# Layer 1's scores for three quarters of the rows: dots on VectorE in place of turns and a four-column product on TensorE

## The chip, the cores and the metric

The kernel runs on one core of a Trainium2 chip. The metric is the device time of one execution in microseconds (us). The core has four compute engines that work side by side, each with its own in-order program: TensorE (PE, products and turns), VectorE (DVE), ScalarE (ACT) and GpSimd (POOL). SyncE (SP) issues DMAs. The engines wait for one another through semaphores.

## The reference, cut to what matters

Four graph layers run one after the other over the same adjacency matrix `adj` (4096 x 4096, f32) and node features `x` (4096 x 128). Each layer normalises the rows of `x`, applies its own operation, and adds the result to `x`.

```python
h = relu(layernorm(x)); x = x + L0(h, adj)       # (inv_deg * A') @ h, a linear map, relu
h = relu(layernorm(x)); x = x + L1(h, adj)       # graph attention, 2 heads
...
# L1, head i; x here is h above
x_norm = ln(x, g1, b1)
h = x_norm @ ff0_w[i].T
s_src = h @ attn_w[i, :c];  s_dst = h @ attn_w[i, c:]
e = leaky_relu(s_src[:, None] + s_dst[None, :])
att = softmax(where(mask, e, NEG), axis=1) @ h + x
```

So every row of layer 1 needs four scores: s_src and s_dst for two heads. Each is linear in the normalised row, so the kernel folds ff0_w, attn_w, g1 and b1 into one 128 x 4 matrix and multiplies each normalised row of 128 values by its four columns. The last of the 128 places carries the constant that b1 needs.

## The kernel before, in words

The 4096 rows are T = 32 blocks of 128, in Q = 4 quarters of S = 8 blocks. A layer works through the quarters. For a quarter `q`, TensorE does 32 steps `k` (function `run`, line 466). In layer 0 a step is 8 products of a 128 x 128 piece of `adj_t` with the 129 columns of block `k` (line 366). Each step's 512 KB of `adj_t` are loaded by SP (line 287) into a ring: 8 places in the first three quarters (`FIRST`), 4 places in the last quarter (`STREAM`), which lie in `ring` and share their space with what layer 1 uses (R in place 0, the tiles E in places 1 to 3).

The load of step k waits until TensorE has used step k-8 (k-4 in the last quarter) and until VectorE has made the mask of that step. VectorE's `masks` (lines 1152 to 1160) writes for each step a uint8 tile that says where `adj_t` is above 0.

All that is not a product or a mask is a hook: a small piece of work that an engine does behind the products or the mask of a given step `k`, in an order written out by hand. In layer 0's quarter q, VectorE's hooks are the rest of quarter q-1's layer 0 (`post0`: divisors, own part, bias, add, self-loops) and its preparation for layer 1 (`feed(1, ...)`: statistics and scales of two normalisations). `stage0` at line 1217 gives their places.

ScalarE writes the normalised rows of quarter q-1 into G[:, 1] (signal `f_norm`). Then, in the kernel before, TensorE turns the 8 blocks (hook 19, line 409), ScalarE copies them from PSUM to U (line 647), TensorE multiplies each by the four columns `qcol` (hook 22, line 420), and ScalarE copies the result into `score1` (line 703, signal `f_placed`).

The last quarter of layer 0 has three things more. VectorE takes the largest score of the first three quarters at step 26 (`early_of`, line 1018). TensorE spreads it over the partitions at hook 25, after a wait for it (`spread_top`, line 453). From it come biases, exponentials on ScalarE, and a spread of rows at TensorE's hook 28 (`spread_rows`). VectorE scales two quarters of G behind the masks 30 and 31 (line 1094). Then layer 1 begins: VectorE makes a tile E for each step (line 1124) and TensorE multiplies it with G (line 382). The scores of the fourth quarter are made in layer 1's first quarter, in the same manner, at TensorE's hooks 17 and 18 of that quarter.

`spare` is the fifth place of `ring`, and holds small weights. `w0T` (layer 0's weights) is its first 128 columns and is not needed after the first quarter; `ff0raw` and `w2raw` lie in the 384 columns behind the other weights, and `affine` and `proj2` lie over parts of them. V is a work tile of 8 x 128 that ScalarE and VectorE share.

Of the kernel before, what the change touches and what calls it, by code (L numbers as in the profile page):

```python
# [64 lines left out]
def graph_layers(nc, x, adj, adj_t, diag, alpha, w0_t, bias0, ff0, ff0_t, ff1_t, attn, g1, b1, g2, b2,  # L65
# [20 lines left out]
    with ExitStack() as ctx:  # L86
# [40 lines left out]
        ff0raw = [spare[:, o + h * D:o + (1 + h) * D] for h in range(HEADS)]  # L127
        affine = ff0raw[1]
        w2raw = spare[:, o + 2 * D:o + 3 * D]
        proj2 = spare[:, o:o + D + 2]  # L130
        mean2 = spare[:, o + D + 2:o + 2 * D + 2]
        fold, later = [spare[:, o + 3 * D + i * S:o + 3 * D + (i + 1) * S] for i in range(2)]
# [52 lines left out]
        f_var, f_dev, f_scale, f_norm = sem("f_var"), sem("f_dev"), sem("f_scale"), sem("f_norm")  # L185
        f2_var, f2_dev, f2_scale, f2_in = sem("f2_var"), sem("f2_dev"), sem("f2_scale"), sem("f2_in")
        h_turned, h_wide, h_projected, h_placed = sem("h_turned"), sem("h_wide"), sem("h_projected"), sem("h_placed")
        f_turned, f_wide, f_projected, f_placed = sem("f_turned"), sem("f_wide"), sem("f_projected"), sem("f_placed")

        top_placed, top_spread, bias_made, row_shifted = sem("top_placed"), sem("top_spread"), sem("bias_made"), sem("row_shifted")  # L190
# [78 lines left out]
        @block.sync  # L269
        def _(sp):  # L270
            def load_x(t, n, loaded):
                sp.dma_start(X[:, t:t + n, :], x[t * P:(t + n) * P, :].rearrange("(s p) d -> p s d", p=P)).then_inc(loaded, 16)  # L272

            def layer0(q, some=range(T)):

                L = STREAM if last_of(q) else FIRST
                for k in some:
                    if k >= L:
                        sp.wait_ge(slot_used, q * (T - 1) + k - L + 1)
                        sp.wait_ge(mask_made, q * T + k - L + 1)  # L280
                    elif 0 < q < Q - 1:
                        if k == L - 1:
                            sp.wait_ge(acc_summed[NB - 1], q)
                        else:
                            sp.wait_ge(slot_used, q * (T - 1) + k - L + 2)
                        sp.wait_ge(mask_made, q * T + k - L + 1)
                    sp.dma_start(tile0(q, k), span(adj_t[k * P:(k + 1) * P, :], q * QC, QC)).then_inc(loaded0(q, k)[0], 16)

            def layer3(q):

                for k in range(T):
                    if not fixed(q):
                        if k == T - 1:
                            sp.wait_ge(acc_summed[NB - 1], q + 2 * Q)
                        else:
                            sp.wait_ge(deep_used, (q - 1) * (T - 1) + k + 1)
                    sp.dma_start(stream3[:, k, :], span(adj[k * P:(k + 1) * P, :], q * QC, QC)).then_inc(deep_loaded[k], 16)

            load_x(0, S // 2, x_first)
            load_x(S // 2, S // 2, x_loaded[0])  # L300
            sp.dma_start(w0T, w0_t).then_inc(w0_loaded, 16)
            layer0(0, range(2))
            load_x(S, S, x_loaded[1])
            layer0(0, range(2, STREAM))
            load_x(2 * S, S, x_loaded[2])
            load_x(3 * S, S, x_loaded[3])
            layer0(0, range(STREAM, T))
            for q in range(1, Q):
                layer0(q)


            sp.wait_ge(back_summed, 1)
            sp.dma_start(proj2[:, 0:D], w2).then_inc(w2_loaded, 16)


            sp.wait_ge(saved, 16 * Q)

            def bring_back(q):
                if fixed(q):
                    sp.wait_ge(post_done, 2 * Q)  # L320
                else:
                    sp.wait_ge(f_turned, q + 2 * Q)
                sp.dma_start(V[:, :, :].rearrange("p s d -> p (s d)"), span(inputs1, q * QC, QC)).then_inc(back, 16)
            bring_back(0)
            quarters(sp, 1, Q - 1, bring_back)

            sp.wait_ge(e_made, 3 * Q * T)
            layer3(0)
            quarters(sp, 1, Q - 1, layer3)
            for b in range(NB):  # L330
                sp.wait_ge(last_made, b + 1)
                some = slice(3 * b, 3 * b + width(b))
                sp.dma_start(out.rearrange("(t p) d -> p t d", p=P)[:, (Q - 1) * S:, :][:, some, :], V[:, some, :])\
                    .then_inc(stored, 16)
            sp.wait_ge(stored, 16 * (Q - 1 + NB))
# [21 lines left out]
        def _(pe):  # L357
# [41 lines left out]

            def feed(h, p, weights, wide, spreads, posts):  # L400

                at = p if h < 3 else p - Q

                def turned():
                    pe.wait_ge(f_norm, p + 1)
                    wait(pe, rows_kept, spreads)
                    if h == 1:
                        for s in range(S):
                            mm = pe.transpose(turn[:, s * P:(s + 1) * P], G[:, 1, (p - Q) * S + s, 0:P], ident[:, :])
                    else:  # L410
                        mm = turn_v()
                    mm.then_inc(f_turned, 1)

                def project():
                    pe.wait_ge(f_wide, at + 1)
                    wait(pe, f_placed, at)
                    wait(pe, post_done, posts)
                    for s in range(S):
                        dst = mix[:, 0, s * 4:s * 4 + 4] if h == 1 else mix[:, s // 3, (s % 3) * PW:(s % 3) * PW + wide]
                        mm = pe.matmul(dst, U[:, s * P:(s + 1) * P], weights, start=True, stop=True, skip_group_check=True)  # L420
                    mm.then_inc(f_projected, 1)
                return turned, project
# [111 lines left out]
                pe.matmul(mix[:, 2, 0:4], affine, qv[:, 0:4], start=True, stop=True, skip_group_check=True)\  # L534
                    .then_inc(back_summed, 1)

            def stage0(q, more={}):
                turned, project = feed(1, Q + q - 1, qcol, 4, 0, q)
                run(0, q, {19: turned, 22: project} | more)
            stage0(1, {3: turn_weights_back, 21: lambda: pe.wait_ge(back_placed, 1)})  # L540
            for q in range(2, Q - 1):
                stage0(q)
            stage0(Q - 1, {25: lambda: spread_top(early_top[1]), 28: lambda: spread_rows(0)})


            def spread_fold():
# [21 lines left out]
            def stage2(q):  # L568
# [6 lines left out]
                if last_of(q):  # L575
                    ks = [1, 11, 12, 25, 26, 27, 29]  
                    run(2, q, at(ks, steps + (lambda: spread_top(early_top[3]), lambda: spread_rows(m))))
                else:
                    ks = [1, 13, 15, 26, 29, 27]  
                    run(2, q, at(ks, steps + (lambda: spread_rows(m, q + 2 * Q),)))  # L580
            stage2(0)
            pe.wait_ge(qv2_placed, 1)
            quarters(pe, 1, Q - 2, stage2)
# [28 lines left out]
        def _(act):  # L612
# [47 lines left out]
            def feed(h, p, q, between=()):  # L660
# [14 lines left out]
                else:  # L675
# [9 lines left out]
                    if h == 1:  # L685
# [1 line left out]
                        act.wait_ge(f2_scale, q + 1)  # L687
                        normalise(lambda s: blocks(G[:, 1, :, :], q, 1, s)[:, 0, 0:D - 1], lambda s: V[:, s, 0:D - 1],
                                  local(scale), local(shift), ACT.Identity, f_norm)
                at = p if h < 3 else p - Q  # L690
                if fixed(p) and p == 0:
                    first_halves()
                    return
                if h == 3:
                    wait(act, half_summed, 0 if fixed(q) and q == 0 else q * 1)
                    widen(f_turned, at + 1, f_wide, halves=True)
                else:
                    widen(f_turned, at + 1, f_wide)
# [153 lines left out]
                feed(0, q, q)  # L852

            def post0(q):
                act.wait_ge(f_turned, q + Q)
                settle()
                act.activation(V[:, :, :], blocks(G[:, 0, :, :], q)[:, :, 0:D], ACT.Copy, scale=restc).then_inc(own_made, 1)
                take(q, later=False)
# [82 lines left out]
        @block.vector  # L941
        def _(dve):
            st = Steps(dve, dve_step)
            STAGE0, STAGE1, STAGE2, STAGE3 = 20, 6, 12, 7
            V3 = V[:, :, :]
            Uf = U3[:, :, 0:D]
            Ud = U3[:, :, D]
# [37 lines left out]
            def feed(h, p, q):  # L985
# [7 lines left out]
                def input_ready():  # L993
                    dve.wait_ge(f2_in, q + 1)

                def second_scales():
                    scales(f2_dev, q + 1, f2_scale, keep=(2, q))

                def halves():
                    dve.wait_ge(f_wide, p - Q + 1)  # L1000
                    wait(dve, half_summed, 0 if fixed(q) and q == 0 else q * 1)
                    dve.scalar_tensor_tensor(hmean, hpart[0], hpart[1], hmean, ALU.add, ALU.add).then_inc(half_summed, 1)
                steps = statistics(lambda s: blocks(X, q, 1, s)[:, 0, :], f_var) + [first_scales]
                if h == 1:
                    half, rest = statistics(of_v, f2_var)
                    steps += [lambda: (input_ready(), half()), rest, second_scales]
                if h == 3:
                    steps += [halves]
                return steps
# [163 lines left out]
            def place_back():  # L1173
# [4 lines left out]
                for c, i in enumerate((1, 3, 0, 2)):  # L1178
                    ins = dve.tensor_copy(qcol[:, c:c + 1], mix[:, 2, i:i + 1])
                ins.then_inc(back_placed, 1)  # L1180
            masks(0, at([0, 1, 2, 6, 7, 9, 14, 15, 17], own_feed(1) + own_feed(2) + own_feed(3)))
            prepare()
            dve.wait_ge(consts_made, 1)
# [32 lines left out]

            def stage0(q, more={}):
                post, fed = post0(q - 1), feed(1, q - 1 + Q, q - 1)
                masks(q, at([2, 3, 5, 6, 18, 7, 8, 10, 12, 13, 15], post + fed) | more)
            stage0(1, {4: place_back})  # L1220
            quarters(dve, 2, Q - 2, stage0, st, STAGE0)
            early = early_of(1)
            stage0(Q - 1, {26: early[0], 28: early[1], 30: lambda: scale_g(1, 0), 31: lambda: scale_g(1, 1)})
# [206 lines left out]
```

## Time and profile before

| | us |
|---|---|
| median of 3 runs | 1242.03 |
| lowest and highest run | 1241.24 and 1245.62 |
| the profiled execution | 1240.94 |
| its span in the trace | 1239.1 |
| PE busy in the span | 1223.0 (99%) |
| DVE busy | 752.7 (61%) |
| ACT busy | 317.8 (26%) |
| layer 0's last three quarters, in the trace | about 79 to 260 |

The profile page is one profiled execution. It gives the busy time of each engine, the chain of work that ended last, the costliest groups of instructions by line, and the DMA issues. A product of f32 shows as two PE instructions. The trace behind it gives each instruction with its start and duration; consecutive instructions of an engine overlap by part of their durations, so the mean duration of one and the distance from one start to the next are two numbers.

### The profile page before, as it was taken

What the parts mean: (1) busy time and instruction counts of PE and PEld (TensorE: products, weight loads), DVE (VectorE), ACT (ScalarE), POOL (GpSimd) and SP (SyncE); (2) the same over time, 40 slices, a digit from 0 to 9 for tenths busy, and PEclk for the clock granted to TensorE, in tenths of its full rate; (3) what the DMA queues carried; (4) which work ended last, traced back from release to release, by engine and by line L of the source; (5) the groups of instructions that cost most, each with busy time, mean ns of one, the idle gap of its engine ahead of it and who ended that gap; (6) DMA issues with size and microseconds to landing.
All of it is one profiled execution on the core that took longest, in us unless ns stands there. A gap on an engine that the chain in (4) does not pass through costs nothing.

```text
span 1239.1 us, 20060 instructions
## 1 busy us (share of the span) xinstructions
PE 1223.0 (99%) x7953; PEld 967.4 (78%) x7953; DVE 752.7 (61%) x1359; ACT 317.8 (26%) x769; POOL 9.6 (1%) x21
## 2 busy tenths in 40 slices
PE   8999999999999999999999999899999999999998
PEld 8999999964444444444454547899999999999998
DVE  5446554588877777778878787778787840000001
ACT  3312121234433324231424144442312130000000
POOL 3000000000000000000000000000000000000000
PEclk9999999999999999999999999999999999999999
DMA  9888886820000000000000000000000069999810
GB/s 315 275 268 285 281 278 215 275 73 1 17 1 17 0 18 0 17 17 1 1 17 0 17 0 18 1 1 1 1 0 1 1 242 409 410 410 398 294 62 18
DMA packets 47241, 144.33 MB, mean 116 GB/s; under 512 B 4784, under 2 KB 13248, under 8 KB 47168
## 3 DMA queue, kind: packets, MB, share of 16 engines
q1 hardware_dynamic: 42976, 139.08, 31.3%
q10 hardware_dynamic: 3696, 3.67, 0.8%
q8 instruction: 52, 0.85, 0.3%
q0 software_dynamic: 496, 0.55, 0.2%
q14 instruction: 21, 0.17, 0.0%
HBM read 139.09 MB, written 4.19 MB: 116 GB/s over the span
## 4 chain that ended last, share of the span: by engine, by line
PE 87%; DVE 7%; DMA 2%; issue 1%; ACT 1%; SPq 1%; DVEq 0%; ACTq 0%
PE acc L366 51%; PE acc L382 30%; DVE ring L1124 4%; PE mix L420 2%; PE mix L448 1%; PE mix L435 1%; PE turn L397 1%; PE turn L393 1%; ACT V L623 1%; DMA mask<-in_adj_t 1%; SPq L272 1%; DMA mask<-in_adj 1%; DVE stats L960 1%; DVE stats L956 0%; DVE X L1273 0%
## 5 line engine op out<-in xcount | busy, mean ns | idle before, releaser
L1124 DVE SCALAR_TENSOR_TENSOR ring<-ring,score,mask 128x1024 f32<-128x1024 f32 x384 | 482.9, 1281 | 113.1 <-PE acc L382 69.5
L382 PE MATMUL acc<-ring,G 128*128 128x512 f32 x1024 | 450.5, 594 | 3.2 <-DVE ring L1124 2.7
L366 PE MATMUL acc<-G,mask 128*128 128x129 f32 x3584 | 403.5, 275 | 1.6 <-DMA mask<-in_adj 1.1
L366 PEld LDWEIGHTS acc<-G,mask 128*128 128x128 f32 x3584 | 401.5, 192 | 2.1 <-DMA mask<-in_adj 1.5
L382 PEld LDWEIGHTS acc<-ring,G 128*128 128x128 f32 x1024 | 189.3, 190 | 234.0 <-issue 201.5
L366 PE MATMUL acc<-G,ring 128*128 128x129 f32 x2560 | 289.8, 275 | 0.3 <-DVE ring L1124 0.3
L366 PEld LDWEIGHTS acc<-G,ring 128*128 128x128 f32 x2560 | 287.8, 192 | 1.5 <-DVE ring L1124 1.2
L1158 DVE TENSOR_SCALAR mask<-mask 128x1024 uint8<-128x1024 f32 x96 | 64.5, 689 | 53.7 <-DMA mask<-in_adj_t 53.5
L1375 DVE TENSOR_SCALAR zero<-U 128x8 f32<-128x8 f32 x3 | 0.5, 171 | 155.0 <-ACT U L816 155.0
L816 ACT COPY U<-acc 128x387 f32<-128x387 f32 (+1 forms) x36 | 15.6, 446 | 270.9 <-PE acc L366 269.9
L635 ACT ACTIVATE dev<-var 128x8 f32<-128x8 f32 x28 | 5.9, 210 | 266.6 <-DVE var L969 266.6
L1158 DVE TENSOR_SCALAR mask<-ring 128x1024 uint8<-128x1024 f32 x32 | 22.0, 692 | 32.1 <-DMA ring<-in_adj_t 22.2
L623 ACT ACTIVATE V<-X,shift,scale 128x128 f32<-128x128 f32 (+1 forms) x92 | 36.7, 481 | 0.0
L775 ACT COPY ring<-turn 128x512 f32<-128x512 f32 x14 | 8.2, 585 | 109.2 <-DVE ring L1124 64.3
L619 ACT ACT_TABLE_LOAD x26 | 33.4, 1283 | 1.2 <-PEq L1409 0.8
L615 ACT COPY cols<-ident 128x1 f32<-128x1 f32 x40 | 7.6, 190 | 95.8 <-DVE shift L979 35.6
L1394 DVE SCALAR_TENSOR_TENSOR zero<-U 128x3 f32<-128x3 f32 (+1 forms) x3 | 0.5, 161 | 50.8 <-ACT U L816 50.8
L623 ACT ACTIVATE V<-U,shift,scale 128x128 f32<-128x128 f32 x64 | 25.5, 481 | 10.3 <-DVE shift L979 10.3
L420 PEld LDWEIGHTS mix<-ring,U 128*128 128x128 f32 x176 | 20.8, 192 | 2.0 <-issue 1.2
L397 PEld LDWEIGHTS turn<-ident,V 128*128 128x128 f32 x120 | 13.7, 141 | 10.0 <-ACT V L623 5.8
L420 PE MATMUL mix<-ring,U 128*128 128x4 f32 (+2 forms) x176 | 21.0, 265 | 0.0
L397 PE MATMUL turn<-ident,V 128*128 128x128 f32 x120 | 15.7, 274 | 4.1 <-ACT V L623 4.1
(168 smaller groups left out, 548.2 us busy)
## 6 DMA issues: line engine op xcount, KB each, us to landing
mask<-in_adj SPq DMA_DIRECT2D x128, 512.0 KB, 14.9
mask<-in_adj_t SPq DMA_DIRECT2D x96, 512.0 KB, 4.7
ring<-in_adj_t SPq DMA_DIRECT2D x32, 512.0 KB, 4.7
inputs<-V ACTq DMA_DIRECT2D x4, 512.0 KB, 2.7
V<-inputs SPq DMA_DIRECT2D x4, 512.0 KB, 3.9
X<-in_x SPq DMA_DIRECT2D x3, 512.0 KB, 10.6
out_x<-V ACTq DMA_DIRECT2D x3, 512.0 KB, 15.1
X<-in_x SPq DMA_DIRECT2D x2, 256.0 KB, 3.2
```

Source lines behind the costliest of these rows:

```text
L272: sp.dma_start(X[:, t:t + n, :], x[t * P:(t + n) * P, :].rearrange("(s p) d -> p s d", p=P)).then_inc(loaded, 16)
L366: mm = pe.matmul(acc[:, b, (s % 3) * DW:(s % 3) * DW + DW], lhs[:, s * P:(s + 1) * P], g, start=(k == 0 and s % 3 == 0), stop=(k == T - 1) ...
L382: mm = pe.matmul(acc[:, c, :], g, moving[:, c * BANK:(c + 1) * BANK], start=(k == 0), stop=(k == T - 1), skip_group_check=True)
L393: return pe.transpose(dst, col.broadcast_to([P, P]), ident[:, :])
L397: mm = pe.transpose(turn[:, s * P:(s + 1) * P], V[:, s, :], ident[:, :])
L420: mm = pe.matmul(dst, U[:, s * P:(s + 1) * P], weights, start=True, stop=True, skip_group_check=True)
L435: mm = pe.matmul(mix[:, s // 3, (s % 3) * DW:(s % 3) * DW + DW], U[:, s * P:(s + 1) * P], back_w[h], start=True, stop=True, skip_group_che ...
L619: act.activation(warm[func], ident[:, 0:1], func)
L623: ins = act.activation(dst(s), src(s), func, bias=add(s), scale=mul(s))
L816: act.copy(U[:, b * 3 * DW:b * 3 * DW + w], acc[:, b, 0:w]).then_inc(acc_taken, 1)
L1124: dve.scalar_tensor_tensor(E[k % EB], R, rank[h][:, k:k + 1], span(mask, (q * T + k) * QC, QC), ALU.max, ALU.mult).then_inc(e_made, 1)
L1158: dve.tensor_scalar(span(mask, (q * T + k) * QC, QC), tile0(q, k), 0.0, None, ALU.is_gt).then_inc(mask_made, 1)
```

## The change

For the quarters 0, 1 and 2 the scores are no longer made by TensorE. VectorE makes them from the rows in G[:, 1] with `scalar_tensor_tensor`: it multiplies the 128 values of a row with the 128 values of one score's column, and sums along the row with `accum_out` into `score1`. That is one instruction for each block and score, 4 x 8 = 32 for a quarter, in four hooks of eight at the steps 18, 20, 21 and 23. The elementwise product goes to V and is not read. The fourth quarter's scores are made as before.

The four columns have to lie along the free axis on all partitions. In layer 0's quarter 1, TensorE spreads them (four transposes of a broadcast column, hook 6), and VectorE copies them into `w0T` and the 384 columns of `spare` (hook 9). The self-loops move from hook 18 to hook 22. The waits that counted `f_turned`, `f_wide` and `f_placed` of layer 1's feeds are renumbered, and the load of `w2` waits for the last dots rather than for `back_summed`.

```diff
+        dot_w = [w0T] + [spare[:, o + i * D:o + (i + 1) * D] for i in range(3)]
...
-            sp.wait_ge(back_summed, 1)
+            sp.wait_ge(f_placed, 2 * Q - 1)
             sp.dma_start(proj2[:, 0:D], w2).then_inc(w2_loaded, 16)
...
-            def stage0(q, more={}):
-                turned, project = feed(1, Q + q - 1, qcol, 4, 0, q)
-                run(0, q, {19: turned, 22: project} | more)
-            stage0(1, {3: turn_weights_back, 21: lambda: pe.wait_ge(back_placed, 1)})
+            def spread_dots():
+                pe.wait_ge(back_placed, 1)
+                for c in range(4):
+                    mm = spread(qcol[:, c:c + 1], mix[:, 0, c * P:(c + 1) * P])
+                mm.then_inc(dots_spread, 1)
+            run(0, 1, {3: turn_weights_back, 6: spread_dots})
             for q in range(2, Q - 1):
-                stage0(q)
-            stage0(Q - 1, {25: lambda: spread_top(early_top[1]), 28: lambda: spread_rows(0)})
+                run(0, q, {})
+            run(0, Q - 1, {25: lambda: spread_top(early_top[1]), 28: lambda: spread_rows(0)})
...
             def post0(q):
-                act.wait_ge(f_turned, q + Q)
+                act.wait_ge(f_placed, q + Q)
...
+                def dots(c):
+                    if c == 0:
+                        dve.wait_ge(f_norm, p + 1)
+                    else:
+                        st.wait()
+                    for s in range(S):
+                        ins = dve.scalar_tensor_tensor(V[:, s, :], blocks(G[:, 1, :, :], q, 1, s)[:, 0, 0:D], 1.0, dot_w[c],
+                                                       ALU.mult, ALU.mult, accum_out=blocks(score1, q, 1, s)[:, 0, c:c + 1])
+                    if c == 3:
+                        ins.then_inc(f_placed, 1)
+                    else:
+                        st.mark(ins)
...
+            def keep_dots():
+                dve.wait_ge(dots_spread, 1)
+                dve.tensor_copy(w0T, mix[:, 0, 0:P])
+                dve.tensor_copy(spare[:, o:o + 3 * D], mix[:, 0, P:4 * P]).then_inc(dots_kept, 1)
+                dve.wait_ge(dots_kept, 1)
...
-                masks(q, at([2, 3, 5, 6, 18, 7, 8, 10, 12, 13, 15], post + fed) | more)
-            stage0(1, {4: place_back})
+                masks(q, at([2, 3, 5, 6, 22, 7, 8, 10, 12, 13, 15, 18, 20, 21, 23], post + fed) | more)
+            stage0(1, {4: place_back, 9: keep_dots})
```

## Rows read from the trace of the kernel before

**Rows 1.** The page: engines' busy time, TensorE's granted clock by slice.
```profile
PE 1223.0 (99%) x7953; PEld 967.4 (78%) x7953; DVE 752.7 (61%) x1359; ACT 317.8 (26%) x769; POOL 9.6 (1%) x21
...
PEclk9999999999999999999999999999999999999999
```

**Rows 2.** Windows, layer 0's last three quarters: PE, PEld, DVE, ACT, POOL busy; clock, DMA share, GB/s.
```profile
80.00:139.00 59.00, 59.00 (x531) 59.00 (x530) 33.04 (x94) 12.51 (x35) 0.00 (x0) 1.00 0.83 277
139.00:199.20 60.20, 60.20 (x542) 60.20 (x541) 30.90 (x84) 13.60 (x39) 0.00 (x0) 1.00 0.78 267
199.20:260.40 61.20, 61.20 (x547) 60.98 (x546) 37.74 (x96) 16.39 (x44) 0.00 (x0) 1.00 0.73 242
```

**Rows 3.** The chain in order of time, last quarter of layer 0: start, length, what.
```profile
235.38 0.87 PE turn L409 x8
...
241.62 1.68 PE mix L420 x16
243.30 5.46 PE acc L366 x48
248.76 0.11 PE mix L393
...
252.48 4.83 DMA ring<-in_adj_t
```

**Rows 4.** Timeline of VectorE in the last quarter: start, length, instruction, idle before.
```profile
199.44 1.90 DVE L1158 TENSOR_SCALAR mask<-ring 128x1024 uint8<-128x1024 f32 x3 [9.78 <-PE acc L366]
...
230.94 0.69 DVE L1158 TENSOR_SCALAR mask<-ring 128x1024 uint8<-128x1024 f32 x1 [0.93 <-DMA ring<-in_adj_t]
231.55 1.70 DVE L1213 TENSOR_TENSOR mask<-mask,ident 128x128 uint8<-128x128 uint8 x8
...
246.70 0.19 DVE L1018 TENSOR_REDUCE cols<-score 128x1 f32<-128x24 f32 x1
...
257.94 1.22 DVE L1094 TENSOR_TENSOR G<-G 128x1024 f32<-128x1024 f32 x1
259.07 2.47 DVE L1124 SCALAR_TENSOR_TENSOR ring<-ring,score,mask 128x1024 f32<-128x1024 f32 x2
```

**Rows 5.** Timeline of ScalarE in the last quarter.
```profile
227.18 3.18 ACT L623 ACTIVATE G<-V,shift,scale 128x127 f32 x8 [2.46 <-DVE norms L982]
```

**Rows 6.** Groups by line: count, busy us, mean ns of one, idle before.
```profile
L1202 DVE TENSOR_TENSOR U<-U,ring 128x1024 f32<-128x1024 f32 x4 | 4.9, 1220 | 1.6 <-ACT U L623 1.6
L1198 DVE SCALAR_TENSOR_TENSOR U<-U,cols,V 128x1024 f32<-128x1024 f32 x4 | 5.1, 1277 | 0.0
L1205 DVE SCALAR_TENSOR_TENSOR X<-U,X 128x1024 f32<-128x1024 f32 x4 | 4.9, 1218 | 0.0
```

**Rows 7.** Timeline of VectorE: eight 128 x 128 operations with two f32 sources.
```profile
1065.22 2.19 DVE L1383 SCALAR_TENSOR_TENSOR V<-U,inv,X 128x128 f32<-128x128 f32 x8
```

**Rows 8.** Timeline of ScalarE: activations that sum along the row, with the sum's read.
```profile
619.03 0.60 ACT L643 ACTIVATE U<-turn 128x512 f32<-128x512 f32 x1 [1.59 <-PE turn L397]
619.52 0.19 ACT L643 ACTIVATION_READ_ACCUMULATOR U<-turn 128x1 f32 x1
619.61 0.59 ACT L643 ACTIVATE U<-turn 128x512 f32<-128x512 f32 x1
```

**Rows 9.** Timeline of VectorE in the quarters 1 and 2.
```profile
87.35 0.34 DVE L1179 COPY ring<-mix 128x1 f32<-128x1 f32 x4
...
162.52 2.07 DVE L1158 TENSOR_SCALAR mask<-mask 128x1024 uint8<-128x1024 f32 x3
```

**Rows 10.** Timeline of ScalarE in quarter 2.
```profile
162.74 3.18 ACT L623 ACTIVATE G<-V,shift,scale 128x127 f32 x8 [1.68 <-DVE norms L982]
```

**Rows 11.** Timeline of TensorE in quarters 1 and 2, and its longest wait later.
```profile
86.64 28.83 PE L366 MATMUL acc<-G,mask 128*128 128x129 f32 x256
...
175.14 1.04 PE L409 MATMUL turn<-ident,G 128*128 128x128 f32 x8
...
802.36 1.09 PE L397 MATMUL turn<-ident,V 128*128 128x128 f32 x8 [2.75 <-ACT V L623]
```

More of the change, by code:

```diff
@@ L187, in graph_layers @@
         h_turned, h_wide, h_projected, h_placed = sem("h_turned"), sem("h_wide"), sem("h_projected"), sem("h_placed")
+        dots_spread, dots_kept = sem("dots_spread"), sem("dots_kept")
         f_turned, f_wide, f_projected, f_placed = sem("f_turned"), sem("f_wide"), sem("f_projected"), sem("f_placed")
@@ L321, in bring_back @@
                 else:
-                    sp.wait_ge(f_turned, q + 2 * Q)
+                    sp.wait_ge(f_turned, q + Q + 1)
                 sp.dma_start(V[:, :, :].rearrange("p s d -> p (s d)"), span(inputs1, q * QC, QC)).then_inc(back, 16)
@@ L400, in feed @@
             def feed(h, p, weights, wide, spreads, posts):
-                at = p if h < 3 else p - Q
+                at = p if h == 0 else Q if h == 1 else p - 2 * Q + 1
                 def turned():
@@ L415, in project @@
                     pe.wait_ge(f_wide, at + 1)
-                    wait(pe, f_placed, at)
+                    wait(pe, f_placed, p if h < 3 else p - Q)
                     wait(pe, post_done, posts)
@@ L579, in stage2 @@
                     ks = [1, 13, 15, 26, 29, 27]
-                    run(2, q, at(ks, steps + (lambda: spread_rows(m, q + 2 * Q),)))
+                    run(2, q, at(ks, steps + (lambda: spread_rows(m, q + Q + 1),)))
             stage2(0)
@@ L689, in feed @@
                                   local(scale), local(shift), ACT.Identity, f_norm)
-                at = p if h < 3 else p - Q
                 if fixed(p) and p == 0:
@@ L693, in feed @@
                     return
+                if h == 1 and not (fixed(p) and p == 2 * Q - 1):
+                    return
+                at = p if h == 0 else Q if h == 1 else p - 2 * Q + 1
                 if h == 3:
@@ L943, in _ @@
             st = Steps(dve, dve_step)
-            STAGE0, STAGE1, STAGE2, STAGE3 = 20, 6, 12, 7
+            STAGE0, STAGE1, STAGE2, STAGE3 = 23, 6, 12, 7
             V3 = V[:, :, :]
@@ L999, in halves @@
                 def halves():
-                    dve.wait_ge(f_wide, p - Q + 1)
+                    dve.wait_ge(f_wide, p - 2 * Q + 2)
                     wait(dve, half_summed, 0 if fixed(q) and q == 0 else q * 1)
@@ L1006, in feed @@
                     steps += [lambda: (input_ready(), half()), rest, second_scales]
+                if h == 1 and not (fixed(p) and p == 2 * Q - 1):
+                    steps += [lambda c=c: dots(c) for c in range(4)]
                 if h == 3:
```

## The prediction

> **What bounds the kernel now.** I read the page first. TensorE is busy for 1223.0 us of the 1239.1 us span, and its granted clock is full in all forty slices [rows 1]. The windows of layer 0's last three quarters say the same of the place of the change: PE fills them, while VectorE has 33.04, 30.90 and 37.74 us in 59.00, 60.20 and 61.20 [rows 2]. So what leaves TensorE's stream there shortens the kernel, as long as nothing makes TensorE wait in its place. The chain in order of time shows what leaves: in each quarter one piece of 0.87 us (eight turns) and one of 1.68 us (eight products, two instructions each), both on the chain [rows 3]. The chain also shows where layer 0 ends: at 252.48 it goes from TensorE to the load of step 31 (4.83 us), then by its mask and the scaling of G to VectorE's first tile E at 259.07 [rows 3, 4]. From there VectorE holds the chain for a while. A shift of TensorE's step 27, which frees that load, is therefore a shift of all that follows. Last I read VectorE's timeline in the last quarter, because it has the most to do there and the ring has only four places.
>
> **TensorE's part.** Removed: three times 0.87 + 1.68 = 2.55 us, together 7.65 us. Added: four transposes of a broadcast column, each as long as the one at 248.76, 0.11 us [rows 3]: 0.44 us. Net 7.21 us less. The four wait for `back_placed` at hook 6 of quarter 1. VectorE places the last column at 87.35 + 0.34 = 87.69; TensorE starts step 4 at 86.64 and has 256 instructions in 28.83 us, 1.80 a step of sixteen, so it comes to the hook at 92.0 [rows 9, 11]. The wait is hidden with 4.3 us to spare. `keep_dots` needs the result only behind mask 9, and its two copies go into VectorE's slack of this quarter.
>
> ScalarE loses two copies and one small copy a quarter; it is idle for three quarters of the time there, so this is worth nothing. SP's `w2` load now waits for the last dots, but SP is still issuing layer 0's last loads then (the one at 252.48 is later [rows 3]), and nothing asks for `w2` before layer 2.
>
> **What one dot costs.** The trace has no sum along the row on VectorE. Its nearest rows: eight `scalar_tensor_tensor` of 128 x 128 with two f32 sources take 2.19 us at 346 ns each, so one starts (2.19 - 0.346) / 7 = 0.263 us behind the other [rows 7]. Those take a scalar from memory; at 1024 columns such an operation takes 1277 ns and one with an immediate 1218 [rows 6], and the dots have an immediate: 0.263 - 0.059 = 0.204. The sum has to be written out. On ScalarE that is an instruction of its own: it starts at 619.52 and the next activation at 619.61, 0.09 us [rows 8]. A dot is then 0.204 + 0.09 = 0.29 us, my value, and eight are 2.32. The low end is 0.204, if the sum is free. The high end is a dot with no overlap at all: 0.346 + 0.19 (the full length of ScalarE's read) = 0.54. I take the low side, since every pipelined row of VectorE has the overlap.
>
> The Trainium skill ("VectorE: DVE Perf Modes", The DRAIN you can't avoid) says that a next operation doesn't start until the pipe is empty. Rows 7 contradict this for plain operations (2.19 us, not 8 x 0.346 = 2.77); for a pair of dot and read no row speaks, and by that rule the kernel would end near the slower rival below.
>
> **Quarters 1 and 2: hidden.** VectorE gets 32 dots, 9.3 us, and has 26 to 29 us idle [rows 2]. It waits for `f_norm` at step 18: in quarter 2 its mask 18 ends at about 163.9 (the second of the three at 162.52), and ScalarE ends the rows at 162.74 + 3.18 = 165.92 [rows 9, 10], so it stands for 2 us, with the masks from 19 on queued behind it. From 165.92, three hooks (6.96), five masks (3.0) and the self-loops (1.6) put mask 23 at 177.5. TensorE, which began the turns behind step 19 at 175.14 [rows 11], would end step 23 without them at about 182.3. The load of step 31 asks for both; TensorE is the later. Even a dot of 0.49 us would only make them equal, and eight places leave seven more steps. So both quarters give their full 2.55 us. The loads then have to come at 512 KB in 1.8 us, 291 GB/s, where the windows have 277 and 267 [rows 2] because the 2.55 us are in them.
>
> **The last quarter: not hidden.** All times here in the clock of the kernel before. VectorE's mask 18 starts when its load has landed, 230.94; `f_norm` is there already (227.18 + 3.18 = 230.36 [rows 5]). From here to the largest score VectorE must do, in order: nine masks (18 to 26) at (1.90 - 0.69) / 2 = 0.605, 5.45 us; four hooks of dots, 32 d for a dot of d us; the self-loops, 1.61 (1.70 less the overlap of 0.09 with the next start); and the reduction with its handover, 0.19 + 0.05 [rows 4]. It is done at 238.24 + 32 d, with d = 0.29 at 247.52. The loads do not hold it: that of step 26 asks for mask 22 (240.93) and lands 4.83 us later at 245.8, and VectorE gets to it at 246.7.
>
> TensorE ended step 25 at 243.30 + 5.46 = 248.76. Less 2.55 this is 246.21, and here it waits for the largest score [rows 3]. The stall is 238.24 + 32 d - 246.21 = 32 d - 7.97, which is 1.31 us. Before, this wait was covered: the reduction started at 246.70, 2.1 us early. Behind it nothing new is late: the load of step 28 asks for mask 24 (246.07), lands at 250.9, and TensorE gets there at 251.2. The end of layer 0 and the first tile E move with TensorE's steps 26 and 27. The last quarter gives 2.55 - 1.31 = 1.24 us.
>
> **Sum.** -7.65 + 0.44 + 1.31 = -5.9 us. In the profiled execution's own time, 1240.94 - 5.9 = 1235.0. The median of the three runs is 1.1 us above that execution, so the forecast of a median is 1236.1. In general the change is 32 d - 15.2 us while the stall is positive, that is from d = 0.25 on: -7.2 (the floor) up to there, -4.6 for d = 0.33, -3.7 for 0.36, +2.1 for the high end 0.54.
>
> **Rivals.**
> 1. *No stall.* If a dot takes 0.25 us or less, VectorE has the score in time and all 7.2 us are gained: 1234.8. For it: the low end 0.204 and the ScalarE read's 0.09 being perhaps less here (four 128 x 1 copies take 0.34 us, of which one is 0.146: 0.065 apart [rows 9]; that gives 0.27). Against: even that leaves 0.6 us of stall. Chance 12%.
> 2. *The sum takes an own pass or a second cycle for each element.* From 128 to 1024 columns the start distance grows by about 1.03 ns a column (1.19 us at 1024, from 2.47 - 1.28 in rows 4, and 0.263 at 128), so 128 columns are 0.13 us; doubled, d = 0.42 and the change is -1.7 us: 1240.3. Against it: at 1024 columns the two-source operation that multiplies and adds takes no longer (1218 ns) than the plain one (1220) [rows 6], but neither sums. Chance 15%.
> 3. *Slower: the dots do not overlap.* Each dot waits for the whole one before it and its read: 0.346 + 0.146 (a single 128 x 1 copy [rows 9]) = 0.49 us, and the stall at step 25's hook is 7.7 us, more than all three quarters give back. The change is +0.5: 1242.5; the point from which it decides is d = 0.475. With rival 2 on top, d = 0.62 and +4.6: 1246.6. For it: the read needs the end of the sum before it. Against: ScalarE's read needs the same and costs 0.09 us. Chance 10%.
> 4. *TensorE's clock falls in the new stall.* The longest wait of TensorE, 2.75 us at 799.6, left the clock full [rows 1, 11], and the stall that I expect is half of that. If it falls for two steps, these cost double, +3.6: 1239.7. Chance 3%.
>
> On rival 2 the Trainium skill ("Vector Engine (DVE) Microarchitecture Reference", Points that are easy to get wrong) says that this form with two non-bf16 SBUF sources runs at half rate, as no port is left to read back the accumulator. The 1218 ns show that it doesn't for operations without a sum; for one with a sum no row here tells. By it the sum would be rival 2's.
>
> **How the numbers follow.** The forecast has the other 60%, with d from 0.26 to 0.36 and a change of -6.9 to -3.7. A measurement can tell about 0.5%, 6.2 us. That is beyond d = 0.28: rival 1 whole, and a good third of the forecast's cases, make 35% for faster. Rivals 2 and 4, most of 3 and the rest make 60% for the same. Slower by 6.2 us needs a dot near 0.67 us or something unforeseen: 5%. The range goes from the floor with a little for the spread of the medians, 1233.8, up to 1241.0, which takes in rival 2 and leaves rival 3 out.
>
> **What would show it.** Right: no L409 and 16 fewer L420 instructions in each of the three quarters; windows of PE 2.5 us shorter in quarter 2; dots of about 0.29 us each, eight in 2.3; one wait of TensorE of 1 to 2 us before the spread at step 25 of the last quarter, put down to VectorE's reduction. Wrong: waits of TensorE for loads in quarters 1 and 2 (then masks are late there), a wait at hook 6, the first tile E later against the last product than now, or dots of over 0.4 us.

## The result, and the profile after

| | before | changed |
|---|---|---|
| median of 8 runs, us | 1242.38 | 1235.58 |
| lowest and highest | 1240.58 to 1245.62 | 1231.05 to 1238.30 |
| profiled execution, us | 1240.94 | 1234.05 |
| its span, us | 1239.1 | 1232.3 |
| ratio to before, with its 95% interval | | 0.9941 [0.9926, 0.9957] |

The changed kernel is faster: by 0.59% (7.3 us) by the ratio of the runs, by 6.8 us by the medians. The forecast was 1236.1 us, a change of -5.9.

The page of the changed kernel, engines' busy time:

```profile
PE 1217.1 (99%) x7885; PEld 961.8 (78%) x7885; DVE 772.2 (63%) x1553; ACT 314.0 (25%) x760; POOL 9.6 (1%) x21
```

TensorE has 5.9 us less and VectorE 19.5 us more [rows 1]. Windows over layer 0's last three quarters (columns as in rows 2). The edge at 139.00 is where quarter 1 ends in the kernel before; here it ends about 2 us earlier, so the second window holds that quarter's gain too:

```profile
80.00:139.00 59.00, 59.00 (x531) 59.00 (x530) 41.13 (x167) 12.10 (x34) 0.00 (x0) 1.00 0.85 289
139.00:194.50 55.50, 55.50 (x499) 55.50 (x498) 36.25 (x143) 11.63 (x33) 0.00 (x0) 1.00 0.79 276
194.50:253.20 58.70, 58.44 (x522) 58.06 (x520) 43.86 (x160) 15.05 (x41) 0.00 (x0) 1.00 0.74 253
```

TensorE still fills the windows. Its timeline at the start of the last quarter, at its new wait and at the start of layer 1:

```profile
194.41 46.62 PE L368 MATMUL acc<-G,ring 128*128 128x129 f32 x416
241.28 0.32 PE L395 MATMUL mix<-ident,cols 128*128 128x128 f32 x1 [0.26 <-DVE cols L1040]
...
253.22 5.46 PE L384 MATMUL acc<-ring,G 128*128 128x512 f32 x12
```

In the kernel before, the last quarter starts at 199.24 and layer 1 at 260.40. So 4.83 us are gained up to the last quarter, which took 61.2 us and takes 58.8. The chain in order of time (start, length, what):

```profile
92.30 0.44 PE mix L395 x4
92.73 142.95 PE acc L368 x1280
...
235.69 4.71 DMA ring<-in_adj_t
...
240.43 0.69 DVE mask L1180
241.12 0.11 DVE cols L1040
...
241.28 0.32 PE mix L395
...
243.42 4.96 DMA ring<-in_adj_t
...
251.89 2.48 DVE ring L1146 x2
```

Three things can be read here. The four spreads cost 0.44 us. From 92.73 TensorE does 80 steps in one piece of 142.95 us, where pieces of 0.87 and 1.68 us stood in between [rows 3]. And in the last quarter the chain leaves TensorE for the load of step 26 (235.69), its mask and the reduction, before the spread of the largest score. Of TensorE's waits in the whole kernel one is new (us in total, times, longest), and one is gone, 1.15 us for a load of layer 3:

```profile
PE mix L395 <- DVE cols L1040: 0.3, 1, 0.3
```

VectorE's timeline in the last quarter, at the first hook of dots and at the largest score (start, length, and in brackets the idle time before):

```profile
226.03 0.70 DVE L1180 TENSOR_SCALAR mask<-ring 128x1024 uint8<-128x1024 f32 x1 [0.73 <-DMA ring<-in_adj_t]
226.64 0.29 DVE L1009 SCALAR_TENSOR_TENSOR V<-G,ring 128x128 f32<-128x128 f32 x1
226.85 0.08 DVE L1009 DVE_READ_ACCUMULATOR V<-G,ring 128x1 f32 x1
226.85 0.29 DVE L1009 SCALAR_TENSOR_TENSOR V<-G,ring 128x128 f32<-128x128 f32 x1
...
228.34 0.69 DVE L1180 TENSOR_SCALAR mask<-ring 128x1024 uint8<-128x1024 f32 x1
...
240.43 0.69 DVE L1180 TENSOR_SCALAR mask<-ring 128x1024 uint8<-128x1024 f32 x1 [0.45 <-DMA ring<-in_adj_t]
241.04 0.19 DVE L1040 TENSOR_REDUCE cols<-score 128x1 f32<-128x24 f32 x1
```

Eight dots take 228.34 - 226.64 = 1.70 us, 0.213 us each. Each dot is two instructions, and the read of the sum starts at the same time as the next dot: it hides beneath it. Before the mask of step 26 VectorE is idle for 0.45 us, until the load has landed: it is not VectorE's work that makes the score late.

### The profile page after: what moved, and what is told of

It reads as the page before. It is cut to its first block, busy times and chain, and to the rows that moved or that the text cites. A ratio compares the mean times of both kernels' runs of the same rounds, so it can differ in the third digit from the quotient of the medians.

```text
span 1232.3 us, 20107 instructions
## 1 busy us (share of the span) xinstructions
PE 1217.1 (99%) x7885; PEld 961.8 (78%) x7885; DVE 772.2 (63%) x1553; ACT 314.0 (25%) x760; POOL 9.6 (1%) x21
## 4 chain that ended last, share of the span: by engine, by line
PE 87%; DVE 7%; DMA 2%; issue 1%; ACT 1%; SPq 1%; DVEq 0%; ACTq 0%
PE acc L368 52%; PE acc L384 30%; DVE ring L1146 4%; PE mix L450 1%; PE turn L399 1%; PE mix L437 1%; PE mix L422 1%; PE turn L395 1%; DMA mask<-in_adj_t 1%; DMA ring<-in_adj_t 1%; ACT V L627 1%; DVE stats L966 1%; SPq L274 1%; DVE stats L962 0%; DVE X L1300 0%
## 5 line engine op out<-in xcount | busy, mean ns | idle before, releaser
L1009 DVE SCALAR_TENSOR_TENSOR V<-G,ring 128x128 f32<-128x128 f32 x96 | 21.3, 287 | 2.7 <-ACT G L627 2.7
L627 ACT ACTIVATE U<-U,inv 128x128 f32<-128x128 f32 x64 | 19.5, 388 | 0.0
```

The source lines that it names most:

```text
L627: ins = act.activation(dst(s), src(s), func, bias=add(s), scale=mul(s))
L1009: ins = dve.scalar_tensor_tensor(V[:, s, :], blocks(G[:, 1, :, :], q, 1, s)[:, 0, 0:D], 1.0, dot_w[c], ALU.mult, ALU.mult, accum_out=block ...
```

## The experiments

Each was timed beside the kernel before on one chip, so the ratios are what is compared. One thousandth is 1.24 us. Each ratio has an interval of 1.4 to 2 us to either side, so the last column, a difference of two ratios, is uncertain by about 2 us.

| kernel | median, us | ratio to before [95%] | against the changed kernel, by ratio |
|---|---|---|---|
| changed | 1235.58 | 0.9941 [0.9926, 0.9957] | |
| e1, TensorE's work put back | 1243.92 | 1.0020 [1.0008, 1.0032] | +9.8 us |
| e2, no dots | 1234.75 | 0.9944 [0.9931, 0.9958] | +0.4 |
| e3, dots twice in the last quarter | 1242.14 | 0.9999 [0.9986, 1.0011] | +7.2 |
| e4, dots twice in quarters 1, 2 | 1234.78 | 0.9947 [0.9932, 0.9961] | +0.7 |
| e5, all four quarters as dots | 1239.81 | 0.9981 [0.9970, 0.9992] | +5.0 |
| e6, hooks moved in the last quarter | 1233.83 | 0.9936 [0.9923, 0.9948] | -0.6 |
| e7, e6 and the turn one step later | 1231.91 | 0.9921 [0.9905, 0.9936] | -2.5 |
| e8, no sum | 1233.15 (one run) | | |

**e1: TensorE's removed work put back.**

```diff
+            def turns_again(q):
+                pe.wait_ge(f_norm, Q + q)
+                ...  # eight transposes of G[:, 1] into turn
+            def products_again(q):
+                pe.wait_ge(dots_kept, 1)
+                ...  # eight products of G[:, 1] with qcol into mix
+            def again(q):
+                return {19: lambda: turns_again(q), 22: lambda: products_again(q)}
-            run(0, 1, {3: turn_weights_back, 6: spread_dots})
+            run(0, 1, {3: turn_weights_back, 6: spread_dots} | again(1))
...          # and the same for the quarters 2 and 3
```

> The changed kernel with TensorE's removed work put back as idle work: at steps 19 and 22 of layer 0's quarters 1 to 3 it turns eight blocks of G[:, 1] and does the eight four-column products again (from G in place of U), and nobody reads them. The dots stay and give the scores. My theory (the gain is the 2.55 us a quarter that left TensorE's stream): time comes back by 7.65 us less the 0.26 us stall that the products then cover, so 7.4 us above the changed kernel and 0.4 above the kernel before (the four spreads). Rival (the gain comes from ScalarE's freed copies or from the moved self-loops and waits): it stays near the changed kernel, within 2 us.

Measured: 9.8 us above the changed kernel and 0.2% above the one before. Its chain in the last quarter, and VectorE's first tile E:

```profile
235.65 0.87 PE turn L547 x8
...
241.89 1.68 PE mix L552 x16
...
252.75 5.06 DMA ring<-in_adj_t
```

```profile
259.57 2.47 DVE L1159 SCALAR_TENSOR_TENSOR ring<-ring,score,mask 128x1024 f32<-128x1024 f32 x2
```

The first tile E comes at 259.57: 7.68 us later than in the changed kernel (251.89) and 0.50 later than before [rows 4]. This is close to the theory's 7.4 and 0.4. So what layer 0 gains is the 2.55 us a quarter; ScalarE's relief and the moved self-loops, which e1 keeps, give nothing that shows there. The time lost 2 us more than that. In this profiled execution they lie near 1007, where TensorE waits for an early load of layer 3, and the granted clock is 0.70 in the window from 1008 to 1012:

```profile
1009.61 10.59 PE L368 MATMUL acc<-G,mask 128*128 128x129 f32 x78 [2.08 <-DMA mask<-in_adj]
```

The kernel before has this wait too (1.15 us). None of the eight profiled executions without TensorE's turns and products in layer 0 has it, neither the changed kernel nor e2 to e8. So 1 to 2 us of the gain may lie there, outside the prediction's sum. One execution of each kernel can't settle it, and why the load is later was not tried.

**e2: no dots.**

```diff
-                    for s in range(S):
-                        ins = dve.scalar_tensor_tensor(V[:, s, :], ..., accum_out=...)
+                    ins = dve.memset(blocks(score1, q)[:, :, c], 0.0)
```

> The changed kernel with each hook of eight dots replaced by one memset of eight zeros into the score column, so the scores of three quarters are left out and VectorE has 20 us less. As the prediction put it, the dots cost a stall of 1.3 us in the last quarter: this kernel would be 1.3 us faster. My present theory (trace of the changed kernel: a dot starts 0.213 us behind the other, the wait at step 25 is 0.26 us and ends with the load of step 26): it is the same as the changed kernel, within 0.3 us, and the wait of 0.26 us at the spread of the largest score is still there, since the ring of four places sets it.

Measured: the same time as with the dots. The wait at the spread is still there; in this execution it is 0.45 us, and TensorE had waited 0.62 us for a load five steps before:

```profile
241.88 0.32 PE L395 MATMUL mix<-ident,cols 128*128 128x128 f32 x1 [0.45 <-DVE cols L1038]
```

The times alone, uncertain by 2 us, could not tell 1.3 us from nothing; the traces can. With the dots VectorE is idle before the mask of step 26, and without them the wait is no shorter: the prediction's 1.3 us for the dots are refuted, and what is left of the stall belongs to the loads of the ring of four places. How much is left differs from execution to execution, though the ring, its loads and the hook are the same: 0.26 us in the changed kernel, 0.45 here, 0.17 in e5, none in e4 and e8.

**e3 and e4: the dots twice, in the last quarter or in the two before it.**

```diff
-                    for s in range(S):
+                    for again in range(2 if fixed(q) and q == Q - 2 else 1):     # e4: if not (...)
+                        if again:
+                            st.then(ins)
+                        for s in range(S):
```

> The changed kernel with each dot of the last quarter of layer 0 done twice (64 in place of 32), so that a dot costs 0.43 us there. Theory (VectorE's stretch from mask 18 to the largest score decides, by 32 d): the stretch takes 5.45 + 1.61 + 0.24 + 64 x 0.213 = 20.9 us from 226.03, the score comes at 247.0, TensorE waits 5.9 us at step 25 and the loads of steps 25 and 26 in front of it take part of that; time 5.0 to 6.0 us above the changed kernel. Rival (VectorE is idle enough, and the work is hidden): 0 to 1 us.

> The changed kernel with each dot of layer 0's quarters 1 and 2 done twice, the last quarter as it is. Theory (eight places in the ring, VectorE ahead of TensorE by 5 us and more): 0, within 0.5 us. Rival (VectorE's masks become late and the loads with them): 2 to 6 us slower, with waits of TensorE for loads in both quarters.

Measured: +7.2 us and +0.7 us. In e4 VectorE is busy 43.27 of the 55.6 us in the window of quarter 2, up from 36.25 of 55.5, and TensorE has no wait in either quarter:

```profile
92.83 102.00 PE L368 MATMUL acc<-G,mask 128*128 128x129 f32 x912
```

```profile
139.00:194.60 55.60, 55.60 (x501) 55.60 (x500) 43.27 (x209) 11.46 (x33) 0.00 (x0) 1.00 0.83 294
```

The extra dots are hidden. In e3 the stall is there as worked out; TensorE's timeline and three windows from the end of the stall on (columns as in rows 2):

```profile
247.45 0.47 PE L395 MATMUL mix<-ident,cols 128*128 128x128 f32 x1 [5.51 <-DVE cols L1043]
247.72 7.17 PE L368 MATMUL acc<-G,ring 128*128 128x129 f32 x48
```

```profile
247.50:249.50 2.00, 2.00 (x10) 2.00 (x11) 0.49 (x1) 0.00 (x0) 0.00 (x0) 0.50 0.90 313
249.50:251.50 2.00, 2.00 (x13) 2.00 (x13) 1.22 (x5) 0.08 (x1) 0.00 (x0) 0.59 0.49 193
251.50:253.50 2.00, 2.00 (x21) 2.00 (x20) 0.72 (x2) 0.58 (x3) 0.00 (x0) 1.00 0.46 119
```

The wait is 5.51 us against 5.9 less a part. Behind it the granted clock is 0.50, TensorE's lower level, and three steps take 7.17 us where they take 5.52 at full clock: 1.65 us that the expectation did not have. This is the prediction's fourth rival, at a stall four times as long as the one it was put for. With it the expected 5 to 6 us become the measured 7. So 32 more dots in the last quarter cost 7 us, and 64 more in the two quarters before it cost nothing that can be measured: it is the place that decides.

**e5: the fourth quarter as dots too.**

```diff
-                if h == 1 and not (fixed(p) and p == 2 * Q - 1):
+                if h == 1:
                     steps += [lambda c=c: dots(c) for c in range(4)]
...
-                    ks = [17, 18, 19, 21, 22, 25, 26]
-                    run(1, q, at(ks, own + (...)))
+                    ks = [19, 21, 22, 25, 26]
+                    run(1, q, at(ks, (...)))
```

> The changed kernel with the fourth quarter's scores made as dots too, at VectorE's hooks 17 to 20 of layer 1's first quarter, and without TensorE's turns and products there (hooks 17 and 18) and ScalarE's copies. Theory (a dot is worth its price only where VectorE has idle time in front of TensorE's next wait; here VectorE holds the chain until step 15 or so and then has about 3.5 us idle up to 300): 32 x 0.213 = 6.8 us more on VectorE, 3.5 of it hidden; 2 to 4 us above the changed kernel although TensorE has 2.55 us less. Rival (what counts is TensorE's work): 2.5 us below it.

Measured: +5.0 us by the ratios (+4.2 by the medians), a little over the upper end. TensorE's timeline in layer 1's first quarter, with its two new waits, and VectorE's before them:

```profile
290.66 5.40 PE L384 MATMUL acc<-ring,G 128*128 128x512 f32 x8 [2.60 <-DVE ring L1148]
299.44 0.32 PE L395 MATMUL mix<-ident,cols 128*128 128x128 f32 x1 [3.38 <-DVE cols L1064]
```

```profile
287.62 0.29 DVE L1011 SCALAR_TENSOR_TENSOR V<-G,ring 128x128 f32<-128x128 f32 x1 [2.06 <-ACT G L626]
```

What the expectation left out is VectorE's own wait: at hook 17 the normalised rows are not there yet, and VectorE stands for 2.06 us with tiles E queued behind. TensorE has 2.55 us less and waits 5.98 more, and in the window 290 to 295 its clock is 0.66: the eight instructions at 290.66 take 5.40 us, where eight take 3.70 at full clock. Together that is 5.98 - 2.55 + 1.70 = 5.1 us, the measured size. The rival, that TensorE's work is what counts, falls.

**e6: the hooks at the end of layer 0.**

```diff
-            run(0, Q - 1, {25: lambda: spread_top(early_top[1]), 28: ...})
+            run(0, Q - 1, {26: lambda: spread_top(early_top[1]), 28: ...})
...
-            stage0(Q - 1, {26: ..., 28: ..., 30: lambda: scale_g(1, 0), 31: lambda: scale_g(1, 1)})
+            stage0(Q - 1, {26: ..., 28: ..., 29: lambda: scale_g(1, 0), 30: lambda: scale_g(1, 1)})
```

> The changed kernel with two moves in the last quarter of layer 0: TensorE's spread of the largest score at hook 26 in place of 25, and VectorE's two scalings of G at hooks 29 and 30 in place of 30 and 31. Theory (the load of step 26 and VectorE's reduction end the 0.26 us wait; behind the load of step 31 the chain goes over mask and scaling to the first tile E): no wait at the spread, 0.26 us; the first tile E starts 1.1 us earlier, and the three waits of TensorE for E (1.3 us) shrink by as much; together 1.0 to 1.4 us below the changed kernel. Rival (the order of these hooks is off the path): 0.

TensorE's timeline:

```profile
243.24 0.27 PE L395 MATMUL mix<-ident,cols 128*128 128x128 f32 x1
...
253.15 9.12 PE L384 MATMUL acc<-ring,G 128*128 128x512 f32 x20
262.53 9.07 PE L384 MATMUL acc<-ring,G 128*128 128x512 f32 x20 [0.26 <-DVE ring L1146]
272.25 14.46 PE L384 MATMUL acc<-ring,G 128*128 128x512 f32 x32 [0.65 <-DVE ring L1146]
```

The wait at the spread is gone, but e4 and e8 have none either with the old hook, so this is not shown to be the move's doing. The first tile E starts at 250.79 in place of 251.89, 1.1 us earlier as expected, but of the three waits for E only the first (0.41 us) goes: the other two stay, and VectorE now waits 0.49 us for ScalarE's copy of layer 0's last sums in front of them. The turn behind step 17 of layer 1 starts 0.5 us earlier. The first row is the changed kernel's turn, the other two are e6's first tile E and its turn:

```profile
287.06 1.04 PE L411 MATMUL turn<-ident,G 128*128 128x128 f32 x8
```

```profile
250.79 2.48 DVE L1146 SCALAR_TENSOR_TENSOR ring<-ring,score,mask 128x1024 f32<-128x1024 f32 x2 [0.21 <-DVE mask L1180]
```

```profile
286.54 1.04 PE L411 MATMUL turn<-ident,G 128*128 128x128 f32 x8
```

Measured -0.6 us by the ratios, below what such a comparison can tell; these rows carry the verdict, and the expected 1.0 to 1.4 was twice too much.

**e7: e6 ("scale_29" below) with the turn of V one step later, in layer 3's first quarter.**

```diff
-            ks = [0, 8, 9, 18, 19, 20, 21, 26, 27]
+            ks = [0, 8, 9, 19, 20, 21, 22, 26, 27]
```

> The kernel of scale_29 with one more move: in layer 2's end (first quarter of the next layer's run) the turn of V, its product and the two spreads behind it go from TensorE's hooks 18 to 21 to 19 to 22, so that TensorE does one more step before it waits for ScalarE's V. Theory (that wait of 2.75 us is long enough for the clock to fall to half in most executions, which costs 1.65 us in the trace of the changed kernel, steps behind it at 0.50): the wait falls to about 1 us, the clock stays full there, and the kernel is 1 to 2 us below scale_29, with little spread between its runs. Rival (only the wait moves, to step 24's scaled sums, and the clock is not the matter): 0 to 0.3 us.

In the changed kernel the clock falls in one place, behind the 2.75 us wait of TensorE for V. The same wait, 2.75 to 2.77 us, stands in nine of the ten traces: behind it the clock fell in six (the changed kernel, e2 to e6) and stayed full in three (the kernel before [rows 11], e1, e8). The wait and a window of the changed kernel, then the window and TensorE's timeline of e7:

```profile
795.37 1.77 PE L399 MATMUL turn<-ident,V 128*128 128x128 f32 x8 [2.75 <-ACT V L627]
```

```profile
795.00:800.00 5.00, 4.63 (x27) 4.63 (x28) 0.29 (x2) 3.05 (x7) 0.00 (x0) 0.66 0.00 2
```

```profile
795.00:800.00 5.00, 4.04 (x36) 4.04 (x37) 1.42 (x2) 3.65 (x9) 0.00 (x0) 1.00 0.01 2
```

```profile
795.96 1.09 PE L399 MATMUL turn<-ident,V 128*128 128x128 f32 x8 [0.97 <-ACT V L627]
...
809.01 5.73 PE L368 MATMUL acc<-G,ring 128*128 128x129 f32 x48 [1.27 <-DVE acc L1106]
```

The wait fell to 0.97 us, and 1.27 us came back at step 24. At full clock that is a gain of 0.5. Measured: 1.9 us below e6, with a mean clock of 1.000 in five of six runs, where e6 had 0.999 in all six. The intervals of the two overlap, so the size is not settled; that the clock stayed up behind this wait is seen in the one trace and fits the means of the runs. With 0.9921 [0.9905, 0.9936] e7 is clearly below the kernel before; 2.5 us below the changed kernel is at the edge of what the comparison can tell, as these intervals overlap too. Its spread, 1230.8 to 1235.6, did not shrink as expected.

**e8: the same multiplications without the sum.**

```diff
-                        ins = dve.scalar_tensor_tensor(V[:, s, :], ..., accum_out=blocks(score1, q, 1, s)[:, 0, c:c + 1])
+                        ins = dve.scalar_tensor_tensor(V[:, s, :], ...)
```

> The changed kernel with the dots' sums left out: the same 96 multiplications of 128 values, without the sum along the row and its read, and one memset of eight zeros into the score column behind each eight, so the scores of three quarters are left out. Present theory (the read of the sum starts together with the next dot and costs nothing): eight start 0.21 us behind each other as with the sum. Rival (the sum costs 0.06 us or more of the 0.213): 0.15 us or less.

```profile
226.47 1.70 DVE L1009 SCALAR_TENSOR_TENSOR V<-G,ring 128x128 f32<-128x128 f32 x8
228.10 0.68 DVE L1181 TENSOR_SCALAR mask<-ring 128x1024 uint8<-128x1024 f32 x1
```

Eight take 228.10 - 226.47 = 1.63 us, 0.204 each, against 0.213 with the sum. The sum and its read cost 0.009 us a dot. The rival falls.

## Why the prediction was right, point by point

- **Where the bound lies: right.** TensorE's stream set the time, and the first tile E moved from 259.07 to 251.89, 7.18 us (e1: back by 7.68).
- **TensorE's part, -7.65 and +0.44: right.** The pieces are gone, the spreads take 0.44 us, and the wait at hook 6 was hidden. Up to the last quarter 4.83 us were gained, where two quarters less the spreads make 4.66.
- **The cost of a dot, 0.29 us: too high, and this is the mis-sized term.** The multiplication was worked out as 0.204 from rows 6 and 7 and measured as 0.204 (e8). The 0.09 us for the read, taken from ScalarE [rows 8], measured 0.009: VectorE starts the next dot together with the read. The dots' floor, "if the sum is free", was the truth, and the words "I take the low side" did not go far enough.
- **Quarters 1 and 2 hidden: right.** Neither has a wait of TensorE, not even with twice the dots (e4).
- **The stall in the last quarter, 1.31 us: wrong in size, and for a second reason.** It is 0.26 us. With d = 0.213 VectorE's own work would have been done 1.15 us early (32 x 0.213 - 7.97); the load of step 26 sets the stall. That load starts when step 22 is used, 235.69, and takes 4.71 us; mask, reduction and handover bring the spread to 241.28, 5.6 us later, where TensorE's three steps take 5.35. Before, the products of hook 22 (1.68 us) stood in these three steps and covered it. The prediction checked this load only against VectorE's late time at d = 0.29 and so took zero stall as the floor for a cheap dot. The loads leave 0 to 0.45 us of stall there, by the execution (e2).
- **VectorE's stretch decides by 32 d where it is long: right.** Twice the dots gave a wait of 5.51 us (e3).
- **The sum.** By its own terms, with the sizes measured, layer 0 gives -7.65 + 0.44 + 0.26 = -6.95, and the first tile E moved by 7.18, where the forecast was -5.9. The whole span moved by 6.8: behind layer 0 the changed kernel's execution lost 1.65 us to the clock at 795 and had no wait for a load of layer 3, where the one before lost 1.15. The prediction has neither of the two. So that the median came within 0.5 us of the forecast is in part luck: the working was 1.3 us short on layer 0, and the runs before had a median 0.35 us above the one it started from.
- **The rivals.** The first (no stall) was nearest, with the right mechanism and 0.26 us left. The second (a sum at half rate) and the third (no overlap) are refuted by 0.213 us a dot. With the second falls, for this case, the Trainium skill's rule of half rate for this form with two f32 sources ("Vector Engine (DVE) Microarchitecture Reference", Points that are easy to get wrong), now also with a sum. With the third falls, for the dots, the Trainium skill's sentence that a next operation does not start until the pipe is empty ("VectorE: DVE Perf Modes", The DRAIN you can't avoid): a dot lasts 0.287 us and the next starts after 0.213. The same paragraph of the Trainium skill adds that a next operation that is not held starts earlier, which the prediction left out; the dots agree with that. The fourth (the clock) did not strike in the new stall of 0.26 us, but did in e3 at 5.51 us.
- **The chances.** "The same" had 0.60 and "faster by over 0.5%" 0.35. The measured 0.59% lies beyond the line, but its interval, 0.43 to 0.74%, has the line in it, so which of the two it was is not settled. At 0.213 us a dot the formula gives -7.2 us, 0.58%: the read's price put the forecast on the near side of the line.

## What to carry to other kernels

Move a small product with few columns from TensorE to sums along the row on VectorE where TensorE is the bound and VectorE is ahead of it: 2.55 us of TensorE against 6.8 us of VectorE was nearly all gain in three quarters and a loss of 5 us in the fourth. Before that, look at which wait of TensorE comes next behind the added work and at what it follows, because the piece that is removed may have covered a load: here 1.68 us of products had hidden the 0.26 us by which a four-place ring is late. And a long wait of TensorE has a second price behind it, when the clock falls.

## What the runs showed of the hardware that I had not expected

- VectorE's read of a sum (82 ns long) starts together with the next operation and costs 0.009 us, while ScalarE's holds its next activation by 0.09 us [rows 8].
- The same wait of TensorE, 2.75 to 2.77 us, left the granted clock full in three executions (the kernel before [rows 11], e1, e8) and not in six (the changed kernel, e2 to e6). In the changed kernel the clock is then 0.50 from 796.0 to 799.0. There the turn, the step and the products up to the next step took 6.15 us (795.37 to 801.52), against 4.50 at full clock (802.36 to 806.86): 1.65 us.
